# A graph layer on one core: node bias taken from fixed rows of the message windows, paired small sums, one block scaled on VectorE, new orders

## The reference

```
em   = concat(x[src], x[dst]) @ msg_w + msg_b
em   = relu(layernorm(em) * msg_g + msg_beta) * edge_weight
msg  = mean of em over the edges that end in a node (0 without an edge)
gate = sigmoid(x @ gate_w + gate_b)
h    = relu(layernorm(concat(x, msg) @ upd_w + upd_b) * upd_g + upd_beta)
out  = layernorm(x + gate * h + (1 - gate) * x)
```

## Time and profile before

| | |
|---|---|
| median of 3 runs | 628.59 us (627.44 to 630.83) |
| profiled execution, its own time | 628.39 us |
| its span, first to last instruction | 626.6 us |
| busy share PE, PEld, DVE, ACT, POOL | 90, 86, 85, 85, 62 % |
| mean granted TensorE clock | 0.971 of 2.4 GHz |
| DMA | 118.44 MB, mean 189 GB/s |

### The profile page before, as it was taken

One profiled execution on the slowest core, in us unless ns is written; L12 is line 12 of the kernel. 1 busy time (PEld: TensorE's weight loads), 2 busy tenths in 40 slices (PEclk: granted clock), 3 DMA queues, 4 the chain that ended last, 5 costly groups with the idle time before them and its releaser, 6 DMA issues.

```text
span 626.6 us, 19668 instructions
## 1 busy us (share of the span) xinstructions
PE 563.5 (90%) x4796; PEld 541.1 (86%) x4796; DVE 529.8 (85%) x2428; ACT 535.7 (85%) x2500; POOL 387.1 (62%) x396
## 2 busy tenths in 40 slices
PE   1364799999999999999999999999999999999771
PEld 0343799999999999999999999999999999999761
DVE  3980158989989899998989989899899999989986
ACT  0021499999999999999999999999999999999883
POOL 1877777777777777777776767677676776300000
PEclk9976799999999999999999999999999999999996
DMA  4213577887878888787887877878787787756642
GB/s 112 64 48 88 136 200 206 208 234 202 231 215 216 221 209 225 204 221 217 217 230 189 226 213 208 230 195 221 210 214 219 204 229 197 208 156 171 182 117 67
DMA packets 199095, 118.44 MB, mean 189 GB/s; under 512 B 15053, under 2 KB 192662, under 8 KB 198934
## 3 DMA queue, kind: packets, MB, share of 16 engines
q1 hardware_dynamic: 184822, 91.95, 52.2%
q0 software_dynamic: 12544, 25.72, 17.2%
q10 hardware_dynamic: 1696, 0.40, 0.3%
HBM read 79.04 MB, written 38.97 MB: 188 GB/s over the span
## 4 chain that ended last, share of the span: by engine, by line
PE 87%; DVE 5%; ACT 5%; issue 2%; DMA 1%; SPq 0%; DVEq 0%; ACTq 0%
PE ps_u L761 14%; PE ps_u L763 13%; PE ps_z L742 9%; PE ps_z L729 7%; PE ps_z L727 7%; PE ps_t L778 7%; PE ps_x L750 6%; PE ps_h L785 6%; PE ps_u L703 3%; PE ps_xs L710 3%; PE ps_xs L736 3%; PE ps_xd L710 3%; PE ps_z L703 2%; DMA halo_i<-in_dst 1%; ACT squares L555 1%
## 5 line engine op out<-in xcount | busy, mean ns | idle before, releaser
L466 POOL DMA_INDIRECT pair_rows<-in_x,gather_idx x392 | 386.9, 987 | 151.5 <-issue 112.9
L761 PE MATMUL ps_u<-u_x_gate,xT 128*128 128x129 f32 x784 | 151.7, 275 | 0.0
L763 PE MATMUL ps_u<-window,onehot 128*128 128x128 f32 x784 | 151.2, 274 | 0.0
L761 PEld LDWEIGHTS ps_u<-u_x_gate,xT 128*128 128x128 f32 x784 | 118.7, 191 | 1.6
L763 PEld LDWEIGHTS ps_u<-window,onehot 128*128 128x128 f32 x784 | 119.0, 192 | 0.0
L588 ACT ACTIVATE un<-ps_u,u_rstd 128x128 f32<-128x128 f32 x392 | 112.0, 372 | 3.2
L1100 DVE TENSOR_SCALAR out_rows<-y,y_small,y_rstd 128x128 f32<-128x128 f32 x392 | 110.5, 355 | 4.6 <-ACT y_rstd L611 4.6
L1048 DVE SCALAR_TENSOR_TENSOR y<-ps_h,gate_small,x_rows 128x128 f32<-128x128 f32 x392 | 109.8, 342 | 1.2 <-PE ps_h L785 1.2
L555 ACT ACTIVATE squares<-ps_u 128x128 f32<-128x128 f32 x392 | 105.7, 288 | 3.0 <-PE ps_u L763 2.9
L555 ACT ACTIVATION_READ_ACCUMULATOR squares<-ps_u 128x1 f32 x392 | 85.6, 219 | 0.0
L1055 DVE BATCH_NORM_STATS2 y_stats<-y 128x6 f32<-128x128 f32 x392 | 84.6, 278 | 0.0
(11 more groups left out here) (133 smaller groups left out, 1119.2 us busy)
## 6 DMA issues: line engine op xcount, KB each, us to landing
window<-rows_scratch SPq DMA_DIRECT2D x196, 129.0 KB
x_rows<-in_x SPq DMA_DIRECT2D x98, 256.0 KB
out<-out_rows SPq DMA_DIRECT2D x98, 256.0 KB
rows_scratch<-msg_rows SPq DMA_DIRECT2D x49, 258.0 KB, 3.1
pair_rows<-in_x,gather_idx POOLq DMA_INDIRECT x392
const_in<-in_constants SPq DMA_DIRECT2D x1, 1037.0 KB, 5.1
rows_scratch<-pad_rows SPq DMA_DIRECT2D x5, 64.5 KB, 2.7
weights<-in_L_gnn_msg_w ACTq DMA_DIRECT2D x1, 128.0 KB, 5.3
```

Source lines behind the costliest of these rows:

```text
L466: return nc.gpsimd.indirect_dma_start(rows[:, j * P:(j + 1) * P], None, x, bass.IndirectOffsetOnAxis(ap=offsets, axis=0))
L761: nc.tensor.matmul(u_tile(j, ROW), tile(xT[b], j), u_x_gate[:], start=False, stop=False, skip_group_check=True)
L763: last = nc.tensor.matmul(u_tile(j, P), tile(onehot[b], j), window[slot][:, j * ROW:j * ROW + P], start=False, stop=True, skip_group_check ...
```

## The change

The update's bias leaves PE. Row 0 of each window buffer now holds the bias in its 128 columns and a node number (2 to the 60th) that the comparison always meets, since row 0 of the places holds the same number; rows 1 to 15 stay zero. A load fills rows 16 to 127, so a tile's window is 112 rows, and the general way is taken where 112 don't hold a tile's edges. The gate's bias becomes the bias operand of ACT's gate instruction. Block 1 of each pair is scaled by one DVE instruction over its four tiles (`u_norms`, both banks at once) in place of four of ACT. The gate sums and y sums of a pair are made together over eight columns (`gate_sums`, `y_sums`), as are `y_ln_of` and `y_rstd_of`; y has four buffers. In SP's new step the windows of block 1 are those of pair c - 2 and the windows of block 0 those of pair c - 1. All four hand-written orders are new, and the walk has one more lag (5 in place of 4 on PE, DVE and SP, 6 on ACT).

```diff
+FIXED = 16
@@ load_window
+                    sp.dma_start(window[slot][FIXED:P, :].rearrange("p (a i h) -> p i a h", i=2, h=ROW)[:, i],
...
+                                     "(a p) h -> p a h", p=P)[0:P - FIXED]).then_inc(win_loaded[slot], 16)
```

```diff
@@ SP: window_free(k, b)
+                wait(sp, u_done, k.at(4, 2 * b - 6))
+                if b == 1:
+                    return
...
@@ SP: step
+                node(store_out, at, 5, 0)
+                node(store_out, at, 5, 1)
+                    load_messages(b, 1, at_b)
+                node(load_x, at, 2, 1)
+                edge(store_rows, at, 0)
+                    load_messages(a, 0, at_a)
+                node(load_x, at, 1, 0)
```

```diff
@@ ACT
-                nc.scalar.activation(gate_exp[b][:].rearrange("p (a t) -> p a t", a=2).unsqueeze(3), u_gates,
-                                     ACT.Exp, scale=-1.0).then_inc(gate_exp_ready, 1)
+                nc.scalar.activation(gate_exp[k.c % 2][:, b].rearrange("p (a t) -> p a t", a=2).unsqueeze(3), u_gates,
+                                     ACT.Exp, bias=gate_bias[:], scale=-1.0).then_inc(gate_exp_ready, 1)
...
@@ ACT: step
+                node(u_rstd_of, at, 5, 1)
+                pair(y_rstd_of, at, 6)
+                edge(z_squares, at, 1)
+                edge(z_ln_of, at, 1)
+                edge(z_rstd_of, at, 1)
+                node(first_squares, at, 4, 0)
+                node(hT_of, at, 5, 1)
+                node(other_squares, at, 4, 0)
+                edge(emT_of, at, 1)
+                node(u_ln_of, at, 4, 0)
+                node(gates, at, 4, 0)
+                node(u_rstd_of, at, 4, 0)
+                node(xT_of, at, 4, 1)
+                node(first_norms, at, 4, 0)
+                node(other_norms, at, 4, 0)
+                edge(xsT_of, at, 0)
+                edge(xdT_of, at, 0)
+                node(hT_of, at, 4, 0)
+                node(first_squares, at, 4, 1)
+                node(other_squares, at, 4, 1)
+                node(xT_of, at, 3, 0)
+                node(u_ln_of, at, 4, 1)
+                node(gates, at, 4, 1)
+                pair(y_ln_of, at, 5)
```

```diff
@@ PE: update and step
-                bias(ps_u[:, a * 512:a * 512 + 2 * ROW], upd_bias)
-                    nc.tensor.matmul(u_tile(j, ROW), tile(xT[b], j), u_x_gate[:], start=False, stop=False,
+                    nc.tensor.matmul(u_tile(j, ROW), tile(xT[b], j), u_x_gate[:], start=True, stop=False,
...
+                node(first_update, at, 4, 0)
+                node(update_transposes, at, 5, 1)
+                node(other_update, at, 4, 0)
+                node(x_transposes, at, 4, 1)
+                edge(message_transposes, at, 1)
+                node(back_transposes, at, 5, 1)
                 edge(dst_transposes, at, 0)
                 edge(message_update, at, 1)
                 edge(src_transposes, at, 0)
+                node(first_update, at, 4, 1)
+                node(update_transposes, at, 4, 0)
+                node(other_update, at, 4, 1)
+                node(x_transposes, at, 3, 0)
                 edge(message, at, 0)
+                node(back_transposes, at, 4, 0)
```

```diff
@@ DVE
+            for s in range(4):
+                last = v.memset(window[s][0:FIXED, :], 0.0)
...
+            for s in range(4):
+                v.tensor_copy(window[s][0:1, :].rearrange("p (j h) -> p j h", h=ROW)[:, :, 0:P],
+                              upd_bias[0:1].unsqueeze(1).to_broadcast([1, T, P]))
...
+            def u_norms(k, b):
+                dve.wait_ge(u_rstd_ready, k.at(2, b + 1))
+                dve.wait_ge(gate_exp_ready, k.at(2, b + 1))
+                wait(dve, un_in, k.at(2, b - 1))
+                v.tensor_tensor(un[b][:].rearrange("p (a t h) -> p a t h", a=2, h=P), u_values,
+                                u_rstd[b][:].rearrange("p (a t) -> p a t", a=2).unsqueeze(3).to_broadcast(
+                                    [P, 2, 2, P]), ALU.mult).then_inc(un_ready, 2)
...
@@ DVE: step
+                node(residual, at, 4, 0)
+                edge(z_norm, at, 0)
+                node(result, at, 5, 0)
+                node(result, at, 5, 1)
+                node(residual, at, 4, 1)
+                edge(rows, at, 0)
+                node(one_hots, at, 2, 0)
+                node(y_halves, at, 4, 0)
+                node(y_halves, at, 4, 1)
+                pair(y_sums, at, 4)
+                node(one_hots, at, 2, 1)
+                node(u_norms, at, 3, 1)
+                pair(gate_sums, at, 3)
```

More of the change, by code:

```diff
@@ L287, in node, with pair @@
                 task(k, b)
+        def pair(task, at, lag):
+            k = at.back(lag)
+            if k.inside(0, NK):
+                task(k)
         def all_edges(eng, task):
@@ L455, in _ @@
                 head()
-                walk(sp, lambda at: step(at, by_window=False), 4)
+                walk(sp, lambda at: step(at, by_window=False), 5)
             with sp.Else():
-                walk(sp, step, 4)
+                walk(sp, step, 5)
             for s in range(2):
@@ L664, in _ @@
                 head()
-            walk(act, step, 5)
+            walk(act, step, 6)
         @block.tensor
@@ L865, in _ @@
                 head()
-            walk(pe, step, 4, unroll=SLOTS)
+            walk(pe, step, 5, unroll=SLOTS)
         @block.vector
@@ L996, in windows @@
                 link(v.tensor_reduce(block_start[:], starts[:, 0:T], AX.X, ALU.min))
[L997 removed]
+                link(v.tensor_scalar(ends[:], ends[:], float(P - FIXED), block_start[:], ALU.subtract, ALU.is_gt))
                 v.tensor_copy(odd[0:NB, 2, 0, 0:T], ends[0:NB])
@@ L1118, in step @@
             def step(at):
+                node(residual, at, 4, 0)
+                edge(z_norm, at, 0)
+                node(result, at, 5, 0)
+                node(result, at, 5, 1)
                 node(residual, at, 4, 1)
-                edge(z_norm, at, 0)
-                node(result, at, 4, 0)
+                edge(rows, at, 0)
+                node(one_hots, at, 2, 0)
+                node(y_halves, at, 4, 0)
                 node(y_halves, at, 4, 1)
-                node(one_hots, at, 2, 0)
-                edge(rows, at, 0)
-                sums(at, 4, 1)
-                node(residual, at, 3, 0)
+                pair(y_sums, at, 4)
                 node(one_hots, at, 2, 1)
-                node(result, at, 4, 1)
-                node(y_halves, at, 3, 0)
-                sums(at, 3, 0)
+                node(u_norms, at, 3, 1)
+                pair(gate_sums, at, 3)
             def sum_by_node():
                 v.memset(xT[0][:], 0.0).then_inc(zeros_ready, 1)
+                for j in range(T):
+                    last = v.tensor_scalar(iota_block[0:1, j * P:(j + 1) * P], iota_row[0:1, :], float(j * P), None,
+                                           ALU.add)
+                link(last)
                 for j in range(T):
@@ L1174, in _ @@
                 head()
-            walk(dve, step, 4)
+            walk(dve, step, 5)
 def constants(n_nodes):
```

245 lines of the change are left out of this document (103 added, 142 removed).

## The result

The changed kernel takes **634.56 us** (631.36 to 637.33) where the kernel before takes 628.62 (627.44 to 630.89): a ratio of 1.0084, interval 1.0062 to 1.0105. It is 0.8% slower, 24 us above the forecast and outside its range. The profiled execution has a span of 630.8 us, against 626.6.

A forecast was written before the change was run, and what follows sets the result against it. PE was taken as the bound at 11.09 us a step; dropping 0.44 of bias matmuls and keeping a 0.27 wait gave 10.65. 45 steps plus filling and emptying made a 608.5 span, 611 us measured; range 602 to 624 (0.8).

The forecast's parts named there:

- rival 4: POOL becomes the bound because gathers wait out two results in one piece: 631 or 674 us; chance 0.04.
- ACT's relief: ACT loses four of eight norms and one each of y_ln and y_rstd: from 10.86 to about 9.6 us a step.
- loads at 4.6 and 5.15: On SP, block 1's two window loads follow two stores of 0.4 each and issue at these us of the step.
- has 4.0 us to land: Block 1's second window load, issued at 5.15, has this long until its reader, which may slip to 9.15.
- rival 3: Block 1's windows land late; result, store, load and one_hots form a ring on SP and DVE: 643 at 4.7 us; chance 0.07.
- The walk: The new order followed across engines from PE's first_update 4,0 at 0: a step of 10.65 us.
- The term of 0.44 for the bias: Four bias matmuls of 0.11 us leave each PE step, directly on the chain: PE's work falls to 10.38.
- the next to complain: ACT, busy 10.86 us of the old step and 0.24 short of it, taken as next bound after PE.
- The DVE term: DVE gains 0.61 us for u_norms and loses 0.56 on small sums: 9.89 becomes 9.9 to 10.0 a step.
- Eight columns in place of four should not show: Doubling the width of DVE's small sums adds no time beside a fixed cost of 0.16 us.
- 0.3 to spare: DVE's slack in the step: y sums done at 8.8, one_hots at 9.5 us, before u_norms ending at 10.5.
- Rival 1: Handoffs slip by 0.1 to 0.15 us at u_norms and first_update 4,1: step 10.9, 622 us; chance 0.18.

The follow-up runs named there:

- windows first: The changed kernel with SP loading block 1's windows ahead of the two stores of the results, not behind them: 626.7 us, 0.9958 of the kernel before.
- two runs on the windows: The changed kernel with block 1's windows loaded ahead of the result stores (626.7 us), or both blocks' windows loaded together behind the stored rows (626.6 us).
- half on DVE: The kernel before with the bias part, plus two tiles of block 1 scaled by one DVE instruction in place of two of ACT: 618.4 us, ratio 0.9817.
- bias alone: The kernel before with only the bias part (bias in row 0, 112 rows loaded, ACT's bias operand), its orders unchanged: 618.3 us, ratio 0.9828.
- sums interleaved: The changed kernel with block 1's windows loaded ahead of the stores, gate and y sums interleaved and behind u_norms: 625.6 us, 0.9944 of the kernel before.
- both bounds: The changed kernel with block 1's windows ahead of the stores, sums interleaved behind u_norms, message_transposes ahead of x_transposes: 626.3 us, 0.9946 of the kernel before.
- both together: The changed kernel with sums interleaved behind u_norms, message_transposes ahead of x_transposes, both blocks' windows loaded together behind stored rows: 626.6 us, 0.9940 of the kernel before.

## Why the prediction was wrong

**What held.** PE's first full message_update came at 82.4 for 82.0. POOL did not suffer from two results in one piece: it is busy for 387.1 us in both kernels, and between 80 and 560 us a gather beside a result takes 0.96 in the mean (111 of them), any other 0.99, so rival 4 is void. The rule of the Trainium skill (SBUF — State Buffer, Who interferes with whom), by which a VectorE instruction in a two-port mode would lock GpSimd out for its whole length, is not seen beside the results; whether they ran in such a mode, no row tells. u_norms is 0.69 long and holds DVE 0.61, as taken from zn. ACT's relief was counted too high: 10.00 a step is left, not 9.6, in part because four norms hold ACT for 1.01 (300.97 to 301.98 in windows first) and not the 1.14 that includes the last one's latency.

**Block 1's windows, 8.0 of the 22.3 us.** The step that failed is "loads at 4.6 and 5.15", so that the second load "has 4.0 us to land". In the long step above PE's first_update 4,0 starts at 199.82; the loads went at 205.5 and 206.1, which is 5.7 and 6.25. The second store, of 0.40, went only at 204.83 (5.0), and 0.28 of SP's register work follows it, which I had not counted. DVE was free for one_hots at 9.4, so the load had 3.2 us and not 4.0; it took 4.09, not 3.6, and one_hots stood 1.17 for it. This is rival 3, in 16 waits, where I had it in every step or in none. It got 0.07, on one row from the quiet start of the kernel; with the two stores ahead of the loads and the ring named in its own text, it deserved more. The two runs on the windows show it.

**The step itself, 11.0 us.** With the windows cured a step is 10.90, not 10.65. The walk counted each block of PE at its bare length. What it missed are 0.07 and 0.11 at the first matmul of two updates, and 0.07, the mean of every second step's 0.14: there the way from zn to emT is 0.08 longer (1.55 for 1.47) and first_update 4,0 starts 0.08 late behind u_norms. In the kernel before the cheap bias matmul stood at the head of each update, and the gap isn't seen there (306.84 to 307.07). The term of 0.44 for the bias was mis-sized with it: with the orders of before PE's shorter steps are 10.74 (half on DVE), so it was worth 0.35 at best, and 0.2 as built (10.89 in bias alone). I had read ACT, at 10.86, as "the next to complain", but with ACT relieved to 95.67% the mean step stayed at 10.89.

The DVE term was mis-sized too: 0.56 taken off for the sums (1.66 to 1.1), where 0.15 went (to 1.51), so 10.38 a step for 9.9 to 10.0. "Eight columns in place of four should not show" was true (interleaved, nine instructions take 0.79 at eight columns and 0.83 at four), and missed the point: in one set each instruction waits for the one before, and the interleaving before had filled those gaps. The 0.4 beyond my count is more than the "0.3 to spare" that I had left DVE. What it cost is not separable in time: without it (sums interleaved, both bounds, both together) the mean step is 10.90 to 10.94 all the same. So lifting DVE's work, PE's wait for emT or both leaves a mean of 10.90; with both lifted, the end of DVE's loop is one part of what holds it, and the rest is open. Rival 1 had the number (10.9, 622) and part of the place: PE does start first_update 4,0 right behind u_norms, or 0.08 late. But it was not this handoff alone: with the sums behind u_norms and interleaved PE hardly waits for u_norms, and the mean step was 10.94.

**The end, 2.9 us.** Pairs without edges take 10.02 (597.46 and 607.48 are the first updates of the last two), not 9.6, and the last one takes 23.3 from there to the end, not 22:

```profile
597.46 0.46 PE L775 MATMUL ps_u<-u_x_gate,xT 128*128 128x129 f32 x2 [1.94 <-DVE un L1060]
...
607.48 0.46 PE L775 MATMUL ps_u<-u_x_gate,xT 128*128 128x129 f32 x2 [1.93 <-DVE un L1060]
```

The old kernel has 10.0 too: without edges a pair is a chain of handoffs, and the work taken off the engines did not shorten it. The pair more at the end I had counted; what I had not done was to price it beside its purpose. It costs 8 to 10 us, and the rearrangement that it pays for returned none: its step with the windows cured is 10.90, that of bias alone 10.89.

**The whole.** In parts of the time before: the bias part -1.7%, the extra lag +1.6%, the windows' place +1.3%, and the rest (ACT's relief, u_norms, paired sums, the new orders) -0.3%; together, before rounding, the measured +0.8%. The last part is what is left over and no run of its own, so the sum is no check.

## What to carry to other kernels

When four engines lie between 85 and 90%, taking work off one can buy little before another closed way through all of them binds: walk every ring with measured start-to-start times, the loop's end included, before summing busy time. Try the part that removes work from the bound engine alone first; here it was worth 1.7% and the rearrangement around it cost 2.6%. A deeper pipeline costs its extra round at the end whether or not the middle gains, and a load belongs ahead of a store that nobody waits for.

## What the runs showed of the hardware

Small dependent instructions on DVE cost by how they wait, not by their width: a set of eight columns holds the engine for 0.71 or 0.80 when each waits for the one before, and two such sets take 0.79 together when interleaved, where four columns took 0.83. The end of a loop on DVE leaves 0.30 to 0.33 us without work, and holds up the next instruction by 0.41; in both together PE waits 0.41 for zn behind it, while in windows first halving these ends changed nothing. A load of 113 KB that stood behind two stores of 256 KB took 4.09 us in a step where its reader could give it 3.2. What makes every second step of the windows-first run 0.14 longer stays open: DVE's loop is not it, and ACT's was not tried alone.
